# Self-attention of a two-layer decoder: values and sums of weights in one packed product

## The reference, cut to what matters

```python
qkv = jnp.einsum('bsd,ed->bse', x, Wqkv)           # x: (32, 128, 128), normalised
q, k, v = jnp.split(qkv, 3, axis=-1)               # each (B, S, HEADS=16, HEAD_DIM=8)
logits = jnp.einsum('bihd,bjhd->bhij', q, k) * scale + pos_bias[None]
attn = jax.nn.softmax(logits, axis=-1)
out = jnp.einsum('bhij,bjhd->bihd', attn, v).reshape(B, S, D)
return jnp.einsum('bsd,ed->bse', out, Wout)
```

## Time and profile before

| | us |
|---|---|
| median of three runs | 1442.98 |
| lowest and highest of them | 1440.08, 1448.82 |
| profiled execution | 1450.22 |
| its span | 1448.4 |
| TensorE busy in the span | 1359.2 (94%) |
| VectorE, ScalarE, GpSimd busy | 917.2, 809.5, 658.9 |
| self-attention loop in the span | about 702 to 936 |

### The profile page before, as it was taken

One profiled execution on the slowest core, in us unless ns is written; L12 is line 12 of the kernel. 1 busy time (PEld: TensorE's weight loads), 2 busy tenths in 40 slices (PEclk: granted clock), 3 DMA queues, 4 the chain that ended last, 5 costly groups with the idle time before them and its releaser, 6 DMA issues.

```text
span 1448.4 us, 38328 instructions
## 1 busy us (share of the span) xinstructions
PE 1359.2 (94%) x14549; PEld 1051.9 (73%) x14549; DVE 917.2 (63%) x2416; ACT 809.5 (56%) x1590; POOL 658.9 (45%) x664
## 2 busy tenths in 40 slices
PE   6999999988999989999789998899999999998997
PEld 4776777767777767887566666778888888875864
DVE  5555555547887864434788887676667766766123
ACT  4555555546787764545477886755555555542521
POOL 3454555444245632016778776633334444443044
PEclk9999999998998999999899999999999999999999
DMA  5021230000756702247000000000000000001323
GB/s 138 20 67 45 68 119 8 13 1 31 276 204 233 269 23 82 81 137 264 22 10 2 2 2 2 15 2 6 6 6 8 12 12 8 9 13 50 116 57 89
DMA packets 97085, 91.56 MB, mean 63 GB/s; under 512 B 21645, under 2 KB 71434, under 8 KB 96650
## 3 DMA queue, kind: packets, MB, share of 16 engines
q1 hardware_dynamic: 92298, 79.66, 17.0%
q0 software_dynamic: 4608, 9.45, 2.1%
HBM read 30.87 MB, written 58.21 MB: 62 GB/s over the span
## 4 chain that ended last, share of the span: by engine, by line
PE 63%; POOL 10%; issue 10%; DVE 7%; ACT 6%; DMA 2%; SPq 1%; POOLq 0%; DVEq 0%; ACTq 0%
PE bank L3308 6%; PE bank L1711 5%; PE bank L3343 5%; PE bank L1695 5%; PE bank L3322 5%; PE bank L3296 4%; PE bank L2681 3%; PE bank L2691 2%; POOL s_p L1346 2%; PE bank L3334 2%; PE bank L998 2%; PE bank L954 2%; PE bank L924 2%; PE bank L1684 2%; PE bank L975 2%
## 5 line engine op out<-in xcount | busy, mean ns | idle before, releaser
L3080 POOL TENSOR_TENSOR s_p<-s_p,s_inverse 128x616 f32<-128x616 f32 x64 | 77.0, 1223 | 200.6 <-DVE s_inverse L3223 200.6
L1459 ACT COPY s_pT<-bank 77x512 f32<-77x512 f32 (+1 forms) x256 | 135.2, 585 | 44.9 <-PE bank L1695 44.7
L1695 PE MATMUL bank<-ident,s_p 128*77 128x128 f32 (+1 forms) x1024 | 141.9, 286 | 10.7 <-ACT s_p L1450 7.7
L1695 PEld LDWEIGHTS bank<-ident,s_p 128*77 128x77 f32 (+1 forms) x1024 | 118.0, 150 | 36.0 <-issue 17.0
L1346 POOL TENSOR_TENSOR s_p<-s_p,s_peak 128x1024 f32<-128x1024 f32 x64 | 121.1, 1898 | 29.9 <-DVE s_peak L1562 29.8
L1450 ACT ACTIVATE s_p<-s_p 128x616 f32<-128x616 f32 (+1 forms) x128 | 110.7, 885 | 24.1 <-POOL s_p L1346 20.1
L3207 DVE TENSOR_REDUCE s_peak<-bank 128x8 f32<-128x616 f32 x64 | 50.7, 792 | 92.3 <-PE bank L3322 92.3
L3138 ACT ACTIVATE s_p<-s_p 128x616 f32<-128x616 f32 x64 | 46.9, 733 | 81.7 <-DVE s_p L3211 81.7
L3308 PE MATMUL bank<-pos_bias,s_ctx 128*32 128x128 f32 x3072 | 90.5, 274 | 1.7 <-ACT s_kT L3118 1.7
L1711 PE MATMUL bank<-s_pT,s_v 77*32 77x128 f32 (+1 forms) x2048 | 72.0, 282 | 18.6 <-DVE x_all L1596 18.0
L1548 DVE TENSOR_TENSOR s_p<-bank,pos_bias 128x1024 f32<-128x1024 f32 x64 | 77.7, 1215 | 18.0 <-PE bank L1684 18.0
(11 more groups left out here) (374 smaller groups left out, 3375.5 us busy)
## 6 DMA issues: line engine op xcount, KB each, us to landing
sorted_tokens<-s_zero SPq DMA_DIRECT2D x4, 5632.0 KB, 19.7
sorted_tokens<-s_zero SPq DMA_DIRECT2D x8, 2560.0 KB, 16.1
routed_tokens<-s_routed SPq DMA_DIRECT2D x24, 256.0 KB, 2.4
s_tokens<-sorted_tokens SPq DMA_DIRECT2D x48, 64.0 KB, 1.8
s_rows<-sorted_tokens SPq DMA_DIRECT2D x48, 64.0 KB, 1.8
x_all<-x SPq DMA_DIRECT2D x8, 256.0 KB, 3.3
w_s_gateup<-s_gateup SPq DMA_DIRECT2D x1, 2048.0 KB
out<-x_all SPq DMA_DIRECT2D x8, 256.0 KB, 2.6
```

Source lines behind the costliest of these rows:

```text
L1459: nc.scalar.copy(pT[0:keys, b % 2, 4 * q:4 * q + 4, :].rearrange("m h t -> m (h t)"), bank[0:keys, flip_bank("p", b, q), :]).then_inc(drai ...
L1695: last = nc.tensor.transpose(bank[0:keys, into, j * T:(j + 1) * T], p[:, b % 2, 4 * q + j, :], core.ident[:, :])
L3080: nc.gpsimd.tensor_tensor(part, part, inverse[:, b % 2, heads].unsqueeze(2).to_broadcast([P, HU, M]), ALU.mult).then_inc(share_ready, 1)
```

## The change

Only the self-attention is changed; the cross-attention keeps its own branch.

- **Weighing.** The product with `ones` goes. `v` gets, behind the eight columns of each head, a ninth that holds 1.0, so that the ninth row of a head's result is its sum of weights. Three heads of nine rows (27 of 32) fit in a lane; they go to columns A. The fourth head of each row group goes to columns B, in a packing of its own: its eight rows, and three copies of its sum on rows 8, 17 and 26. There are sixteen 128x32 products a batch in place of 32.
- **Sums.** A new VectorE instruction, `spread_sums` (a `stream_shuffle` over 256 columns, from PSUM to SBUF), copies in each lane the sum of each head to all rows of that head. It waits for the weighing, and stands between `peak_of(step,0)` and `add_bias(step,1)`.
- **Inverse and multiplication.** Ln, Exp and the multiplication of `head_outputs` work on 256 columns in place of 128. Ln now reads SBUF in place of PSUM, and waits for the shuffle.
- **Output.** Two 128x128 products that add up, one for columns A and one for columns B, with the rows of Wout laid out accordingly (its tile is 128x256, filled with zeros).
- **Order on ScalarE.** `keep_pT(step-1,1)` comes ahead of `exp_of(step,0)`.
- **Memory.** `inverse` and `oT` move into the tile of a weight that is no longer needed. Before the loop GpSimd clears one larger `v` and sets six single columns to one, in place of clearing `ones` and `v`.

```diff
+HEAD_ROWS = DH + 1
+HEAD_STRIDE = LANE + HEAD_ROWS
+LAST_HEAD = (LANES - 1) * HEAD_STRIDE
+SUM_ROWS = [min(row // HEAD_ROWS, LANES - 2) * HEAD_ROWS + DH for row in range(LANE)]
...
+def spread_rows(woT):
+
+
+    rows = np.zeros((P, 2, D), np.float32)
+    for r in range(LANES):
+        for j in range(LANES):
+            first = LANE * r + HEAD_ROWS * (j % (LANES - 1))
+            rows[first:first + DH, j // (LANES - 1)] = woT[(LANES * r + j) * DH:(LANES * r + j + 1) * DH]
+    return rows
...
+        def clear_packed():
+            nc.gpsimd.memset(v[:, :, :, :], 0.0).then_inc(cleared, 2)
+            pool.wait_ge(cleared, 2)
+            lanes = v[:, :, :, :].rearrange("p n g c -> p (n g) c")
+            for column in range(DH, LAST_HEAD, HEAD_STRIDE):
+                nc.gpsimd.memset(lanes[:, :, column:column + 1], 1.0)
+            for column in range(LAST_HEAD + DH, LAST_HEAD + LANE, HEAD_ROWS):
+                last = nc.gpsimd.memset(lanes[:, :, column:column + 1], 1.0)
+            last.then_inc(ones_ready, 1)
...
         def inverse_of(b):
-            act.wait_ge(weighed, b + 1)
-            if b:
-                act.wait_ge(o_ready, b)
-            nc.scalar.activation(inverse[:, :], bank[:, WORK, B:B + T], ACT.Ln).then_inc(log_ready, 1)
+            act.wait_ge(spread_ready, b + 1)
+            nc.scalar.activation(inverse[:, :], inverse[:, :], ACT.Ln).then_inc(log_ready, 1)
...
+            if b >= 0:
+                keep_pT(b, 1)
             if not cross and 0 <= b < BATCH - 1:
                 exp_of(b + 1, 0)
-            if b >= 0:
-                keep_pT(b, 1)
...
+        def spread_sums(b):
+            dve.wait_ge(weighed, b + 1)
+            if b:
+                dve.wait_ge(o_ready, b)
+            nc.vector.stream_shuffle(inverse[:, :], bank[:, WORK, A:B + T], SUM_ROWS).then_inc(spread_ready, 1)
...
-            nc.vector.tensor_tensor(oT[:, b % 2, :], bank[:, WORK, A:A + T], inverse[:, :],
+            nc.vector.tensor_tensor(oT[:, b % 2, :], bank[:, WORK, A:A + T if cross else B + T], inverse[:, :],
...
                 peak_of(step, 0)
+            if 2 <= step < BATCH + 2 and not cross:
+                spread_sums(step - 2)
+            if 0 < step < BATCH and not cross:
                 add_bias(step, 1)
...
+            if not cross:
+                for j in range(LANES):
+                    at_column = B if j == LANES - 1 else A
+                    first = LAST_HEAD if j == LANES - 1 else LANE * j
+                    for r in range(LANES):
+                        last = nc.tensor.matmul(
+                            bank[LANE * r:LANE * (r + 1), WORK, at_column:at_column + T],
+                            v[:, b % G, r, first:first + LANE], pT[:, b % 2, LANES * r + j, :],
+                            start=(j in (0, LANES - 1)), stop=(j >= LANES - 2), tile_position=(0, LANE * r))
+                last.then_inc(weighed, 1)
+                return
...
+            if not cross:
+                nc.tensor.matmul(bank[:, WORK, OUT], oT[:, b % 2, A:A + T], t["o"][:, 0, :], start=True, stop=False)
+                nc.tensor.matmul(bank[:, WORK, OUT], oT[:, b % 2, B:B + T], t["o"][:, 1, :], start=False,
+                                 stop=True).then_inc(out_done, 1)
+                return
```

More of the change, by code:

```diff
@@ L1185, in narrow_weights @@
     for name in ("q", "k", "v", "o"):
-        t[name] = w.load(s, f"w_{s}_{name}", [P, D], a[f"{s}_w{name}T"])
+        t[name] = w.load(s, f"w_{s}_{name}", [P, 2, D] if s == "s4" and name == "o" else [P, D], a[f"{s}_w{name}T"])
     if s == "s2":
@@ L1260, in narrow_attention @@
     weighed = sem(s + "_weighed")
+    spread_ready = sem(s + "_spread_ready")
     log_ready = sem(s + "_log_ready")
@@ L1372, in by_gpsimd @@
             before.spent(pool)
-            clear_values()
+            clear_packed()
         first_own = 1
@@ L1442, in keep_v @@
             nc.scalar.copy(
-                v[0:keys, :, :, :].rearrange("m n g (j c) -> m (n g) j c", c=STEP)[:, :, :, 0:DH],
+                v[0:keys, :, :, :].rearrange("m n g (j c) -> m (n g) j c", j=LANES)[:, :, :, 0:DH],
                 bank[0:keys, flip_bank("v", g), :].rearrange("m (x j d) -> m x j d", j=LANES,
@@ L1780, in main @@
             pT = late("_pT", [P, 2, H, T])
[L1781 to L1784, removed]
+            if cross:
+                inverse, oT = late("_inverse", [P, T]), late("_oT", [P, 2, T])
+            else:
+                inverse = folded(w.s1_wk, 0, 2 * T)
+                oT = folded(w.s1_wk, 2 * T, 4 * T).rearrange("p (b c) -> p b c", b=2)
+            v = late("_v", [P, G, LANES, LANES * (STEP if cross else HEAD_STRIDE)])
+            if cross:
+                ones = late("_ones", [P, LANES * STEP])
             if cross:
@@ L4078, in laid_out @@
         out[f"s4_w{name}T"] = f["L1_attn_Wqkv"][k * D:(k + 1) * D].T
-    out["s4_woT"] = f["L1_attn_Wout"].T
+    out["s4_woT"] = spread_rows(f["L1_attn_Wout"].T)
     out["ramp"], out["s4_coeffsT"], out["s4_wposT"] = ramp_constants(), f["L1_attn_coeffs"].T, f["L1_attn_Wpos"].T
```

## The result

| | before | changed |
|---|---|---|
| median, us (20 runs each) | 1443.01 | 1448.66 |
| ratio with its 95% interval | | 1.0037 [1.0027, 1.0048] |
| span of the profiled execution | 1448.4 | 1446.8 |

One of the changed kernel's twenty executions took 2248.87 us at a granted clock of 0.555, in a slower state that the ratio leaves out; the other nineteen took 1445.3 to 1453.3. The change makes the kernel 0.4% slower, 3.9 to 6.9 us by the interval. The forecast was 1444, no change by the 1% bound, with a range of 1435 to 1455. The spans stand the other way round because the first trace of the kernel before came from an execution 7 us above its median. So lengths inside the self-attention are compared from here on, not spans.

The account below looks back on a forecast made before the run. The prediction took a chain of one weighing, ScalarE and GpSimd, not TensorE, to close each 26.56 us lap. Its terms, 1.1 - 0.7 + 0.6 + 0.4 = +1.4 us on 1442.98, gave 1444, range 1435 to 1455.

Parts of the forecast that it names:

- What bounds the lap: Four-batch lap of 26.56 us in self-attention: closed by waits through ScalarE and GpSimd, not by TensorE's 95% busy share.
- The floor of 0.39 us a lap: Most a lap could gain if the shuffle's wait is hidden, 26.17 us; as a rival 20%, time 1440.
- one chain: Weighing to v copy 3.08, ScalarE 11.78, GpSimd 9.39, exponential and transposes to next weighing; sums to 26.56 us, one weighing.
- The terms: Prices of the changed parts in us: weighing 0.87 less; Ln and Exp 0.417 each, multiplication 0.42, shuffle 0.42.
- The lap worked out: Replay of one four-batch lap: the shuffle's wait delays GpSimd's subtraction, and the lap grows 0.25 to 26.81 us.
- The stall: After TensorE's stall at 872 us the weighing runs at half clock and is on the path: -0.7 us.
- The steps without projections: Five steps after the stall, 5.70 us each, become 5.92 by a two-step loop: +1.0 at most, +0.6 taken.
- The tail: Last three steps, run serially: +0.19 us each from the changed parts' durations, less what overlaps, +0.4 in all.
- The clock: Rival, 4%: TensorE's busy share falls from 95% to 85% in the laps and brings half clock, time 1459.
- The first group: Self-attention before about 740 us: results of the sublayer before set the pace, so no change.
- a shuffle of 1.35 us: Shuffle length beyond which the kernel would be more than 1% slower; dear shuffle making VectorE the bound: rival, 8%.
- The sum: Whole effect: 1.1 laps, -0.7 stall, 0.6 unprojected steps, 0.4 last steps, together +1.4 us.

Follow-up runs that it names:

- before_no_sums: Kernel before without the sixteen products with ones for every batch but the first, nothing else changed; 1439.13 us, ratio 0.9987.
- after_no_spread: Changed kernel without its shuffle: ScalarE reads the 256 columns straight from PSUM by a scaled copy in place of Ln; 1442.21 us, ratio 1.0002 to the kernel before.
- after_rstd_later: Changed kernel with GpSimd's inverse deviation for the next group moved one step later; 1451.33 us, ratio 1.0060 to the kernel before.
- before_rstd_later: Kernel before with GpSimd's inverse deviation for the next group moved one step later; 1443.92 us, ratio 1.0006.
- after_tail_warm2: Changed kernel with sixteen more products, read by nobody, behind each of the last two weighings; 1448.36 us, ratio 1.0037 to the kernel before.

## Why the prediction was right, point by point

- **What bounds the lap.** Right where it counted: TensorE at 95% busy was not the bound, and before_no_sums shows it without anything else being changed. The floor of 0.39 us a lap below the old one was 0.54 in after_no_spread. Wrong in the sentence that TensorE is busy "beside it, not the cause of it". Steps 3 to 0 to 1 carry a second chain of the same length that holds the weighings. The prediction followed one chain back and stopped when its sum matched the lap. A sum that matches does not exclude a second chain with the same sum.
- **The terms.** Weighing -0.87, Ln and Exp 0.414 and 0.417 (0.417 taken), multiplication 0.414 (0.42), shuffle 0.449 (0.42). The separate instruction for the selection exists, as the page "Vector Engine (DVE) Microarchitecture Reference" of the Trainium skill says in its section 3.8, but it took 0.014 us, not the 0.154 that the smallest row of VectorE had given for it.
- **The lap worked out.** 26.81 forecast, 26.65 measured, so of the 0.25 forecast a lap 0.1 came; the next weighing 6.6 us on, measured 6.58; shuffle, second add, subtraction, exponential and keys came in the order and with the waits described.
- **The stall.** -0.7 forecast, -0.4 against the second trace and -0.9 against the first; two traces of one kernel differ there by 0.5.
- **The steps without projections.** +0.6 forecast; +0.3 from step 28 to 31. The loop over two steps (5.92) measured 5.86.
- **The tail.** The mis-sized term: "less what overlaps, +0.4" for the last steps. From step 31 on it was +1.9. The sum counted durations and left out the queues. The three intervals behind step 31 grew by 0.7, 0.5 and 0.7. In the first, the shuffle, the second add and the second maximum stand ahead of the multiplication in VectorE's queue, and TensorE waits 2.00 us for it against 0.64. In the second, Ln starts 0.4 us after its shuffle, behind a copy on ScalarE, and the second output product adds its 0.22. In the third the forecast of +0.19 would hold at full clock, but both output products ran at half clock: 1.26 us from the first one's start to the add, against 0.75 at full clock and 0.52 before.
- **The clock.** Taken as a rival of 4% in the laps, where it stayed at 1.00, as forecast. It fell in a place that the prediction did not look at, the hand-over to the next stage, and cost 1.7 us there. The prediction compared rows of the laps and of idle stretches, and none of the tail.
- **The first group.** Taken as nothing; +1.3 us, and up to 3.7 in traces of kernels that are the same there. after_rstd_later and before_rstd_later reached step 5 in 42.1 and 41.0 us, where the changed kernel and the kernel before took 43.7 and 42.8, so GpSimd's leg matters there. Without the shuffle the first group takes 69.3 us, as before; but before_no_sums has no shuffle and takes 70.6. So what makes the group longer stays open.
- **Two readings.** Of TensorE's 12.8 us of waits ahead of a weighing, the prediction puts most in one stall; the row gives 4.5 us for the longest. And by its own prices a shuffle of 1.35 us makes 1453 to 1455, which is less than 1% more. With a shuffle of 0.449 us neither mattered.
- **The sum.** +1.4 forecast, about +5.1 by the traces, +5.6 by the medians: sign right, within 1%, size too small by the tail, the hand-over and the first group. That the change is worth nearly nothing where TensorE sheds 2.3 us a lap was understood. The sign is partly luck: the sum owed its +1.4 to +1.1 in the laps, which came to about +0.4, and the loss that was measured lies at the two ends, which it put at +0.4 and nothing.

## What to carry to other kernels

Before valuing work removed from the busiest engine, cut the steady part where it repeats and find the chain that closes one lap; then look for a second chain of the same length before trusting the first, because shortening one of two tied chains gave nothing here. A reduction that is moved from a nearly free place (a product whose rows already stood spread) to an engine in the middle of its queue costs its own time and the wait in front of it, and everything queued behind. Look at both ends of a loop as well as at its laps: the serial tail pays each added link in full, and a longer gap on TensorE there was followed here by half the clock in the next stage. And a trace of each version is one sample: take a second of the same kernel before reading half a microsecond.

## What the runs showed of the hardware that was not expected

A shuffle of 128x256 float32 from PSUM took 0.449 us, 8% more than the multiplication of the same size, and its preceding selection load 0.014 us. In the changed kernel's tail the granted clock was 0.91 over 4 us in which TensorE was busy 1.56, with single waits of no more than 2 us and a weighing between them, and 0.50 (1.2 GHz) over the next 4 us. In the kernel before, busy 2.54 of 4 us with the last wait at 1.11 us, and in after_tail_warm2, busy 2.51 of 4 us, it stayed at 2.4 GHz. Columns that nobody reads were enough to keep it there.
